# A perceiver block on one Trainium2 core: the first transfers in another order, key positions and mask in one transfer

## What is computed

```python
x = x + _L0_xattn_ref(_layernorm(x), ctx, ctx, W_q, W_k, W_v, W_o, itok_8, itok_1, mask)
...
dist = (query_pos[:, :, None] - key_pos[:, None, :]).astype(scores.dtype)
bias = -_slopes(NUM_HEADS)[None, :, None, None] * dist[:, None, :, :]
scores = jnp.where(mask[:, None, :, :] == 0, -jnp.inf, scores + bias)
m = jnp.max(scores, axis=-1, keepdims=True)
e = jnp.exp(scores - m)
attn = e / (1.0 + jnp.sum(e, axis=-1, keepdims=True))
```

## Time and profile before

| what | value |
|---|---|
| median of 3 runs | 753.41 us (752.69 to 754.79) |
| span of the profiled execution, first to last instruction | 751.1 us |
| the profiled execution's own time | not listed apart from its span |
| mean granted clock of TensorE | 0.948 |
| PE busy | 88% |
| DVE, ACT, POOL busy | 65%, 49%, 41% |
| DMA queues, share of 16 engines | SP's 22.8%, GpSimd's 6.0%, ACT's 0.5% |

### The profile page before, as it was taken

One profiled execution on the slowest core, in us unless ns is written; L12 is line 12 of the kernel. 1 busy time (PEld: TensorE's weight loads), 2 busy tenths in 40 slices (PEclk: granted clock), 3 DMA queues, 4 the chain that ended last, 5 costly groups with the idle time before them and its releaser, 6 DMA issues.

```text
span 751.1 us, 16917 instructions
## 1 busy us (share of the span) xinstructions
PE 662.8 (88%) x6115; PEld 500.4 (67%) x6115; DVE 485.5 (65%) x1367; ACT 365.0 (49%) x992; POOL 310.1 (41%) x458
## 2 busy tenths in 40 slices
PE   4899999999999989985994799988999776999990
PEld 3677878787777778753443586667877673777760
DVE  2686777677768669885488873558888875333330
ACT  1454545545555479874395653436566431222320
POOL 1235455646453179850000031136556513556541
PEclk9999999999999999996997699999999986999995
DMA  8723222322220000019200434538001022243434
GB/s 265 245 62 79 64 78 65 78 65 75 68 72 14 1 3 4 3 44 332 103 0 1 156 125 177 217 125 367 2 3 65 3 99 53 47 69 58 68 40 70
DMA packets 31697, 65.08 MB, mean 87 GB/s; under 512 B 5792, under 2 KB 21792, under 8 KB 29312
## 3 DMA queue, kind: packets, MB, share of 16 engines
q1 hardware_dynamic: 26016, 55.73, 22.8%
q0 software_dynamic: 4688, 7.18, 6.0%
q10 hardware_dynamic: 912, 1.10, 0.5%
HBM read 57.67 MB, written 7.37 MB: 87 GB/s over the span
## 4 chain that ended last, share of the span: by engine, by line
PE 64%; DVE 21%; ACT 5%; issue 4%; DMA 2%; SPq 2%; POOL 1%; DVEq 0%; ACTq 0%; POOLq 0%
PE psum L2627 7%; PE psum L474 6%; PE psum L482 6%; PE psum L496 5%; PE psum L2637 4%; PE psum L521 4%; PE psum L507 4%; PE psum L1482 3%; PE psum L1459 3%; PE psum L837 2%; DVE ff_peak L1500 2%; PE psum L846 2%; PE psum L829 2%; PE psum L877 2%; DMA wn<-in_w_down 2%
## 5 line engine op out<-in xcount | busy, mean ns | idle before, releaser
L415 ACT ACTIVATE prob<-s_sb,negm 128x257 f32<-128x257 f32 x128 | 66.2, 517 | 94.5 <-DVE negm L640 94.5
L782 POOL TENSOR_SCALAR bias<-dist,cst 128x257 f32<-128x257 f32 x128 | 59.8, 486 | 99.5 <-DVE dist L627 89.6
L636 DVE CUSTOM_DVE_ANT_0 s_sb<-psum,bias 128x257 f32<-128x257 f32 x128 | 49.4, 423 | 51.7 <-PE psum L496 48.4
L474 PE MATMUL psum<-ctxT,shared 128*128 128x257 f32 x256 | 62.6, 388 | 2.7 <-DMA msk<-in_mask 2.7
L482 PE MATMUL psum<-shared,ctxT 128*128 128x256 f32 x256 | 60.4, 379 | 0.0
L2627 PE MATMUL psum<-ex_w,shared 128*128 x184 | 58.3, 460 | 0.6 <-ACT shared L2520 0.6
L1721 POOL TENSOR_TENSOR wn<-wn,cst 128x1 f32<-128x1 f32 x8 | 4.7, 589 | 120.4 <-DVE wn L1848 120.4
L474 PEld LDWEIGHTS psum<-ctxT,shared 128*128 128x128 f32 x256 | 47.2, 195 | 9.0 <-issue 3.4
L482 PEld LDWEIGHTS psum<-shared,ctxT 128*128 128x128 f32 x256 | 48.4, 189 | 6.8
L496 PE MATMUL psum<-kT,qbd 64*128 64x257 f32 x256 | 48.4, 429 | 3.0 <-DVE mx L636 2.9
L2627 PEld LDWEIGHTS psum<-ex_w,shared 128*128 128x128 f32 x184 | 33.1, 190 | 15.4 <-issue 0.8
(11 more groups left out here) (359 smaller groups left out, 1655.9 us busy)
## 6 DMA issues: line engine op xcount, KB each, us to landing
ctxT<-in_ctx_T SPq DMA_DIRECT2D x32, 257.0 KB
ex_w<-in_w SPq DMA_DIRECT2D x1, 5632.0 KB, 17.5
kpos<-in_kpos SPq DMA_DIRECT2D x32, 128.5 KB
msk<-in_mask SPq DMA_DIRECT2D x32, 128.5 KB
near_turned<-in_ctx_T_tiles SPq DMA_DIRECT2D x4, 1028.0 KB
ff_used_up<-in_ctx_T_tiles SPq DMA_DIRECT2D x4, 1028.0 KB
near_rows<-in_ctx_tiles SPq DMA_DIRECT2D x4, 1024.0 KB, 8.0
ff_used_up<-in_ctx_tiles SPq DMA_DIRECT2D x4, 1024.0 KB, 7.3
```

Of the source, the lines that this page charges most:

```text
L415: nc.scalar.activation(prob[n % 2][:, g, :], s_sb[n % 2][:, g, :], ACT.Exp, bias=negm[:, b, g:g + 1], accum_out=esum[t % 2][:, b, g:g + 1]) \
L474: ins = nc.tensor.matmul(kv[m][:, 0:SK], w["xa_k"][:, k, P * m:P * m + P], ctxT[n % BT][:, k, :], start=(k == 0), stop=(k == KT - 1))
L636: nc.vector.tensor_tensor_reduce(s_sb[n % 2][:, g, :], sc[g % 2][:, 0:SK], bias[n % 2][:, g, :], 1.0, float("-inf"), ALU.add, ALU.max, mx[ ...
L782: nc.gpsimd.tensor_scalar(bias[n % 2][:, g, :], dist[n % 2][:], c.slope[:, g:g + 1], 1.0, ALU.mult, ALU.mult).then_inc(bias_ready, 1)
```

## The change

Key positions and mask of a context become one tile `pos[b]` of [128, 2, 257] integers, loaded by one transfer from an array that the host has already repeated over the partitions, and counted on a semaphore of its own (`keys_known[b]`). PE waits for `ctxT[b]` alone. The four transfers of query positions become one, from a repeated array. The constants move from second on SP's queue to first on ACT's. Tile 1 of `x` gets a transfer and a semaphore of its own (`second_loaded`) behind context 1; tiles 2 to 7 follow behind context 3. DVE waits for the constants only after the first norm, for tile 1 at n = 0 and for tiles 2 to 7 at n = 4.

```diff
-        msk = [sb(f"msk{b}", [P, SK], I32) for b in range(BT)]
-        kpos = [sb(f"kpos{b}", [P, SK], I32) for b in range(BT)]
+        pos = [sb(f"pos{b}", [P, 2, SK], I32) for b in range(BT)]
...
             sp.dma_start(x[:, 0, :], a["x"][:, 0, :]).then_inc(first_loaded, 16)
-            sp.dma_start(cst[:], a["cst"]).then_inc(cst_loaded, 16)
...
                 sp.dma_start(ctxT[b][:], a["ctx_T"][n]).then_inc(ctx_loaded[b], 16)
-                sp.dma_start(kpos[b][:], a["kpos"][n].unsqueeze(0).broadcast_to([P, SK])) \
-                    .then_inc(ctx_loaded[b], 16)
-                sp.dma_start(msk[b][:], a["mask"][n].unsqueeze(0).broadcast_to([4, SQ, SK])) \
-                    .then_inc(ctx_loaded[b], 16)
+                sp.dma_start(pos[b][:], a["key_pos"][n]).then_inc(keys_known[b], 16)
 
             context(0)
-            sp.dma_start(x[:, 1:NT, :], a["x"][:, 1:NT, :]).then_inc(x_loaded, 16)
-            for n in range(1, BT):
+            context(1)
+            sp.dma_start(x[:, 1, :], a["x"][:, 1, :]).then_inc(second_loaded, 16)
+            for n in range(2, BT):
                 context(n)
+            sp.dma_start(x[:, 2:NT, :], a["x"][:, 2:NT, :]).then_inc(x_loaded, 16)
...
+            act.dma_start(cst[:], a["cst"]).then_inc(cst_loaded, 16)
             load("xa_k")
             load("xa_q")
-            for h in range(4):
-                act.dma_start(qpos[SQ * h:SQ * h + SQ, :], a["qpos_T"]).then_inc(pos_loaded, 16)
+            act.dma_start(qpos[:], a["qpos_T"]).then_inc(pos_loaded, 16)
...
-            pe.wait_ge(ctx_loaded[0], 48)
+            pe.wait_ge(ctx_loaded[0], 16)
...
-                    pe.wait_ge(ctx_loaded[b], 48 * (t + 1))
+                    pe.wait_ge(ctx_loaded[b], 16 * (t + 1))
...
-                dve.wait_ge(ctx_loaded[b], 48 * (n // BT + 1))
+                dve.wait_ge(keys_known[b], 16 * (n // BT + 1))
...
-            dve.wait_ge(cst_loaded, 16)
             dve.wait_ge(first_loaded, 16)
             norm_stats(0)
             norm(0)
+            dve.wait_ge(cst_loaded, 16)
             dve.wait_ge(pos_ready, 1)
             distances(0)
             spread_queries(0)
-            dve.wait_ge(x_loaded, 16)
             for n in range(N + 3):
                 t, b = n // BT, n % BT
+                if n in (0, BT):
+                    dve.wait_ge((second_loaded, x_loaded)[t], 16)
...
-            pool.wait_ge(pos_loaded, 64)
+            pool.wait_ge(pos_loaded, 16)
...
-        "qpos_T": i["itok_BxS_8_8191"].T,
-        "kpos": i["itok_BxS2_1_8191"],
-        "mask": i["mask_BxSxS2_if1"],
+        "qpos_T": np.tile(i["itok_BxS_8_8191"].T, (4, 1)),
+        "key_pos": np.stack([np.broadcast_to(i["itok_BxS2_1_8191"][:, None, :], (NB, P, SK)),
+                             np.tile(i["mask_BxSxS2_if1"], (1, 4, 1))], axis=2),
```

More of the change, by code:

```diff
@@ L320, in distance_attention @@
         sc, pt, kv, oo, misc = bank[0:2], bank[2:4], bank[4:6], bank[6], bank[7]
-        ctx_loaded = [sem(f"ctx_loaded{b}") for b in range(BT)]
+        ctx_loaded, keys_known = ([sem(f"{name}{b}") for b in range(BT)] for name in ("ctx_loaded", "keys_known"))
+        second_loaded = sem("second_loaded")
         cst_loaded, wn_loaded, pos_loaded = sem("cst_loaded"), sem("wn_loaded"), sem("pos_loaded")
@@ L622, in distances @@
                 b = n % BT
-                dve.wait_ge(ctx_loaded[b], 48 * (n // BT + 1))
+                dve.wait_ge(keys_known[b], 16 * (n // BT + 1))
                 at_least(dve, bias_ready, 4 * (n - 2) + 4)
-                st.done(nc.vector.tensor_scalar(dist[n % 2][:], kpos[b][:], qposf[:, n:n + 1], None, ALU.subtract))
-                st.link(dve, nc.vector.tensor_scalar(shut[:], msk[b][:], 0.0, -BIG, ALU.is_equal, ALU.mult))
+                st.done(nc.vector.tensor_scalar(dist[n % 2][:], pos[b][:, 0, :], qposf[:, n:n + 1], None, ALU.subtract))
+                st.link(dve, nc.vector.tensor_scalar(shut[:], pos[b][:, 1, :], 0.0, -BIG, ALU.is_equal, ALU.mult))
                 nc.vector.scalar_tensor_tensor(dist[n % 2][:], shut[:], BIG, dist[n % 2][:], ALU.mult, ALU.add) \
```

## The result

The changed kernel takes 749.75 us in the median of 15 runs (746.4 to 750.72), the kernel before 754.15 in 15 (750.21 to 755.4). The ratio is 0.9944, with a 95% interval of 0.9928 to 0.996, that is 3.0 to 5.4 us; the medians differ by 4.4 us. Timed once more, the same kernel gave 0.9939 (0.9922 to 0.9956). The profiled execution took 749.07 us, with a span of 747.3 instead of 751.1.

What follows compares the result with a forecast made beforehand. Transfers were taken to bound only the start, before 34.67 us, through w_down's landing and the work before `scales(0)`; engines bound the rest. Earlier keys 4.0 plus removed idle 0.9 us took 753.4 to 748.5 us, range 746.6 to 750.8.

Steps and rivals of the forecast that it cites:

- its first case: Landing of w_down by 23.6 us, full gain of 4.9 us: likeliest 748.5 us, range 747.2 to 749.5, chance 0.52.
- The first norm and the first keys: Kernel start: DVE's statistics at 4.2 us, transposes at 6.35, PE's first keys at 7.0 instead of 11.03, gaining 4.0 us.
- The stretch to `scales(0)`: From first keys to DVE's `scales(0)`: 16.2 us without transfer waits, shifting as a block to end at 23.2 us.
- The term for the clock: First eight key matmuls, early ones at half rate: taken as 0, with up to 1.3 us sooner possible.
- The landing of w_down: Transfer that `scales(0)` waits for: lands at 22.4 us instead of 28.57, hidden with 0.8 us to spare.
- two bounds 3.6 us apart: For w_down's landing: 24.2 us at the old windows' rates, 20.6 us at a steady 370 GB/s.
- The reading behind it: Transfers up to w_down: the mask's runs on four engines of 16 only, so w_down ends on a few engines.
- The other reading: Dip at 6 to 7 us, 88 GB/s beside the first repeated row, spoke for a landing between the bounds.
- The rivals with a landing of 24.2 or later: w_down's landing: old rates 24.2 us, chance 0.18; 24.4 to 26.2, 0.18; 27 to 28.6, no gain, 0.09; 31.4, slower, 0.03.
- 2 us for a write receipt: Behind w_down's last bytes: the skill's fixed DMA cost, not added to 22.4 us, priced within the later-landing rival, chance 0.18.
- The 1.32 us of idle: DVE's removed wait for w_down at `scales(0)`: worth 0.9 us to PE at its scores of context 2.
- The rest of the run: Contexts 4 to 31 and later stages: no further gain or added work; clock scatter 1 us on either side.

Runs made afterwards that it cites:

- e1: The kernel before with only the semaphores parted, so PE waits for ctxT alone; transfers and their order stay old: ratio 1.0002, 754.94 us.
- e3: The changed kernel with only positions and mask put back to their two old transfers, on their own semaphore: ratio 0.9999 to the kernel before, 754.65 us.
- e9: The changed kernel run once more, with nothing altered: ratio 0.9939 to the kernel before, 749.68 us.
- e2: The kernel before with only positions and mask joined into one transfer of the new shape, on the old semaphore: ratio 0.9947, 750.12 us.
- e4: The changed kernel with two transfers: mask from host-repeated rows, positions from one row repeated over 128 partitions: ratio 0.9926 to the kernel before, 748.86 us.
- the warmed kernel: The changed kernel plus six PE multiplications on a zeroed tile while PE waits for the first transfers: ratio 0.9923 to the kernel before, 748.02 us.
- e11: The changed kernel plus six early PE multiplications on a zeroed tile, timed a second time: ratio 0.9909 to the kernel before, 747.35 us.

## Why the prediction was right, step by step

**The time.** 748.5 us were forecast and 749.75 measured, inside the range of 746.6 to 750.8 and 0.25 us above the 749.5 of its first case. Of the 1.25 us between them 0.7 are no fault of a step: the kernel before took 753.4 us in the three runs that the forecast started from and 754.15 in the fifteen of the result. At scores 2 the gain was 4.4 us of 4.9: the keys gave 0.1 us more than forecast, the stretch behind them 0.2 less, the removed idle time 0.4 less.

**The first norm and the first keys.** Right within 0.1 us. DVE started at 4.13 (4.2 forecast), the transposes at 6.28 (6.35), the keys in the chain at 6.94 (7.0). `xa_k` landed at 1.17 + 4.8 = 6.0, behind its forecast of 5.7 and still early.

**The stretch to `scales(0)`.** It took 23.40 - 6.94 = 16.5 us instead of 16.2. The term for the clock was taken as 0 with 1.3 us sooner as its only bound, and it came out on the other side. The keys were as slow as before, and the rise of the clock now fell into the queries: L464's matmuls took 421 ns at most against 276 before, and the group 1.48 us against the 1.05 of the warm queries at 30.90. The first line is of the changed kernel, the second of the kernel before, min/median/max:

```profile
L464 PE MATMUL psum<-xT,shared x8: 275/346/421, 10.2 to 11.4; 128*128 128x128 f32 x8
```

```profile
L466 PE MATMUL psum<-xT,shared x8: 273/275/276, 14.3 to 15.1; 128*128 128x128 f32 x8
```

That this stretch "holds no wait for a transfer" was true of the trace and not of the work: e1 and e3 show that the masks of contexts 0 and 1 stood right behind the wait that was removed. Where the forecast asks what would hold the gain back if only the first wait went, it names the landing of w_down alone. The sum held because the same change made the masks even.

**The landing of w_down.** 22.1 us, forecast 22.4, and hidden as forecast. That it is so near is partly luck: 22.4 was the middle of two bounds 3.6 us apart, and with the same bytes ahead of it w_down landed at 21.3 in e9, the same kernel, and at 20.6 in e2. The count of issues in the forecast is off by one: SP issues 14 transfers up to and with w_down instead of 18, which changes nothing. The reading behind it, four engines at a share of 0.26 and 0.29, agrees with e2 and e3, which try the mask from both sides. The other reading, that the dips of repeated rows spoke for an earlier landing, was wrong in its weight: e4 has the dip and lands at 22.3. The rivals with a landing of 24.2 or later did not come.

Neither did 2 us for a write receipt: the Trainium skill's fixed cost in "DMA: Bandwidth & Descriptors", "Anatomy of one DMA — SWDGE (gpsimd) path", would have put the landing at 24.4. That section is on transfers that GpSimd issues; these are SP's. The windows up to w_down's landing, on which the forecast leaned, cannot settle it, because later transfers of the queue move bytes in them too. Where a context's two transfers run alone they can: in the changed kernel `pos` was issued at 82.23 and landed 3.0 us later, at 85.2, and its last bytes moved between 84.61 and 84.86, 0.4 to 0.6 us before (windows):

```profile
84.61:84.86 0.25, 0.25 (x5) 0.25 (x4) 0.25 (x3) 0.00 (x0) 0.25 (x1) 1.00 0.22 74
84.86:85.11 0.25, 0.25 (x5) 0.25 (x3) 0.25 (x2) 0.00 (x0) 0.17 (x1) 1.00 0.00 0
```

**The 1.32 us of idle.** Forecast 0.9 us for PE, measured 0.5: from the point where DVE was ready for `wmax` to scores 2 it was 34.67 - 27.25 = 7.42 us and is now 30.30 - 23.40 = 6.90. The step that failed for most of it is the start of the maximum at the end of `spread_queries`. There are 0.28 us between the two, in which DVE waits for its own result; the row of the changed kernel names it, and in the earlier trace rows the same 0.28 us stood under POOL's name.

**The rest of the run.** Forecast as a shift without loss. At the first transposes of the quantised weights (L1431), some 300 us later, all 4.4 us are still there: they start at 321.9 instead of 326.3. When the last twelve of them start 3.9 us are left, and at the last one 3.2, because these now run at a granted clock of 0.50 (330 to 333 us). The first line is of the kernel before, the second of the changed one:

```profile
L1432 PE MATMUL psum<-cst,wn x12: 272/340/417, 334.2 to 335.9; 128*128 128x128 f32 x12
```

```profile
L1431 PE MATMUL psum<-cst,wn x12: 417/417/473, 330.3 to 332.7; 128*128 128x128 f32 x12
```

Over 325 to 335 us the granted clock was 1.00 before and 0.67 after (windows, the kernel before first):

```profile
325.00:335.00 10.00, 7.90 (x107) 6.04 (x106) 9.20 (x15) 7.45 (x20) 4.13 (x7) 1.00 0.00 0
```

```profile
325.00:335.00 10.00, 7.89 (x56) 5.39 (x55) 8.84 (x28) 5.80 (x14) 3.46 (x6) 0.67 0.34 89
```

This is no steady price of the change. The 15 runs of the changed kernel have mean clocks of 0.945 to 0.952; its spans are 744.6 and 746.0 at 0.952, 746.2 and 746.4 at 0.950, and 747.0 to 748.9 in the eleven others, at 0.945 to 0.948. The forecast put 1 us on either side for it; the 15 runs lie from 3.4 us below their median to 1.0 above, and those of the kernel before from 3.9 below to 1.3 above. From the profile alone the gain is 3.8 us; the ratio's 4.2 us, over all runs, is the better number.

Whether the short spans of 744.6 to 746.4 us can be made the rule stays open; nothing was tried on the later stages.

## What to carry to other kernels

A transfer whose source begins with a small repeated dimension can sit on a quarter of the DMA engines, and its price is then paid not only by those who wait for it but also by later transfers in the same queue; look for windows with a DMA share near 0.25, and for the large transfer behind them that is waited for. Before a wait is taken away, work out which semaphore the same data counts on next: here 2.7 us of wait for the mask were worth nothing until the mask itself came earlier. And an order of transfers that is slack for one kernel can be the bound of the next faster one, as x's second tile was once PE had been warmed up.

## What the runs showed of the hardware

In a microsecond in which one row of 1028 bytes was read 128 times, the DMA engines moved 178 GB/s at full share, against 356 for distinct rows in the same microsecond of another run. Four engines of 16, at a share of 0.26, moved 90 GB/s. The granted clock of TensorE fell to half behind early waits in e1, e3 and one of the two profiles of the warmed kernel, with PE busy for 2.5 of the 5 us in which it fell in e1 and for 4.4 of the 5 us before it in e11. At the start of the kernel the granted clock reads 1.00 while matmuls of one shape take 767 ns and later 381 ns, so there the half rate shows in the durations only. Matmuls on zeros served as well as matmuls on data to end it: the slowest of their twelve records took 797 ns and the fastest 380, and the keys behind them took 380.
